# An attention and feed-forward kernel: an earlier load of x, and ScalarE's high halves behind the exponents

## The reference

```python
x = x + xattn(layernorm(x), ctx, ctx, Wq, Wk, Wv, Wo)     # 16 heads of 32, rotary q and k, softmax over 120 keys
x = x + ffn(layernorm(x), w_gate, w_up, w_down)           # 512 -> 1536 -> 512

def ffn(x, w_gate, w_up, w_down):
    x = act_qdq(x)                                        # 16-bit quantize and back, one scale for the tensor
    up = act_qdq(x @ lpbq_dequant(w_up).T)                # 4-bit weights in blocks of 32
    gate = act_qdq(x @ lpbq_dequant(w_gate).T)
    gate = act_qdq(gate * fixed_qdq_u16(sigmoid(gate)))
    return act_qdq(gate * up) @ lpbq_dequant(w_down).T
```

## Time and profile before

| | us |
|---|---|
| median of three runs | 2319.28 |
| the profiled execution | 2318.47 |
| its span, first to last instruction | 2316.7 |
| TensorE busy | 2199.2 |
| VectorE busy | 1686.2 |
| ScalarE busy | 1330.6 |
| GpSimd busy | 704.9 |

### The profile page before, as it was taken

The page is one execution under the profiler, slowest core; times in us unless marked ns, Lnnn a source line. Parts: engine busy times, 40 slices in busy tenths (PEclk is TensorE's granted clock), DMA queues, the critical chain, the costliest instruction groups (busy, mean ns, idle before and its releaser), DMA issues. The chain is left out here.

```text
span 2316.7 us, 31161 instructions
## 1 busy us (share of the span) xinstructions
PE 2199.2 (95%) x12037; PEld 970.5 (42%) x12037; DVE 1686.2 (73%) x1690; ACT 1330.6 (57%) x1299; POOL 704.9 (30%) x655
## 2 busy tenths in 40 slices
PE   5898999999988899999999999999998799999999
PEld 3443333333332444444444444444443344444444
DVE  7656899898975766445543598888888887778773
ACT  3345666666644232222322787877877777777772
POOL 3444675766663311000100364444444000000000
PEclk9899999999999999999999999999999899999999
DMA  6334686877777568888875898877876565655552
GB/s 193 95 103 116 179 194 173 193 173 192 170 159 178 164 215 256 272 246 253 250 227 180 292 329 311 299 286 286 293 284 259 189 234 211 236 226 205 205 217 91
DMA packets 287190, 500.14 MB, mean 216 GB/s; under 512 B 187980, under 2 KB 190284, under 8 KB 250172
## 3 DMA queue, kind: packets, MB, share of 16 engines
q1 hardware_dynamic: 287036, 498.10, 68.1%
HBM read 247.75 MB, written 186.58 MB: 187 GB/s over the span
## 5 line engine op out<-in xcount | busy, mean ns | idle before, releaser
L1698 PE MATMUL banks<-XB,W 128*128 128x512 f16 x2304 | 500.1, 380 | 2.3 <-ACT XB L1724 2.3
L1698 PE MATMUL banks<-XB,WT 128*128 128x512 f16 x2304 | 497.4, 379 | 0.0
L2164 PE MATMUL banks<-W,OH 128*128 128x512 f16 x2256 | 487.1, 379 | 3.6 <-DVE OH L2266 3.6
L1718 ACT ACTIVATE OB<-banks,uns 128x512 f32<-128x512 f32 x384 | 255.7, 684 | 393.2 <-PE banks L1698 390.4
L1698 PEld LDWEIGHTS banks<-XB,W 128*128 128x128 f16 x2304 | 225.9, 98 | 276.1 <-issue 5.1
L1698 PEld LDWEIGHTS banks<-XB,WT 128*128 128x128 f16 x2304 | 225.4, 98 | 271.8
L2164 PEld LDWEIGHTS banks<-W,OH 128*128 128x128 f16 x2256 | 220.7, 98 | 270.0 <-DVE OH L2266 4.0
L1985 POOL TENSOR_TENSOR PR<-GS,OB 128x2048 f32<-128x2048 f32 x46 | 220.5, 4794 | 257.6 <-ACT OB L1718 247.6
L1807 DVE TENSOR_REDUCE amx<-OB 128x1 f32<-128x2048 f32 x48 | 109.7, 2285 | 239.8 <-ACT OB L1718 239.8
L752 PE MATMUL banks<-XC,AH 128*128 128x512 f16 x768 | 179.2, 385 | 5.4 <-POOL AH L1510 3.7
L693 PE MATMUL banks<-XD,WQ 128*128 128x512 f16 x768 | 177.0, 380 | 2.2 <-ACT WQ L878 0.8
(11 more groups left out here) (272 smaller groups left out, 2866.2 us busy)
## 6 DMA issues: line engine op xcount, KB each, us to landing
g_s<-OB SPq DMA_DIRECT2D x48, 1024.0 KB, 6.0
GL<-g_s SPq DMA_DIRECT2D x48, 1024.0 KB, 7.3
up_s<-OB SPq DMA_DIRECT2D x48, 1024.0 KB, 4.9
XA<-up_s SPq DMA_DIRECT2D x32, 1024.0 KB, 9.3
gq_s<-GQ SPq DMA_DIRECT2D x48, 512.0 KB, 4.7
XD<-gq_s SPq DMA_DIRECT2D x48, 512.0 KB, 6.7
XA<-in_x SPq DMA_DIRECT2D x16, 1024.0 KB, 6.3
QW<-QE SPq DMA_DIRECT2D x128, 128.0 KB, 3.0
```

What stands on the lines that cost most here:

```text
L1698: t = e.matmul(pk[:].rearrange("p (j t) -> p j t", j=4), WT[w][:, ot, wa, kk, :], XB[i % 2][:, xa, :, kk, :], start=(kk == 0 and wa == 0 a ...
L1718: e.activation(OB[n % 3][:, r, :], bank[(k + 4) % 8][:], ACT.Copy, scale=uns[:, 12 * w + ot:12 * w + ot + 1]).then_inc(s_ev, 1)
L2164: t = e.matmul(pk[:].rearrange("p (r n) -> p r n", r=4), OH[i % 2][:, a, ot, j * 128:(j + 1) * 128], WD[:, :, c, wa, o4, :], start=(ot == ...
```

## The change

For steps s >= 16, five things move:

- SyncE issues the load of x in c = 1, ahead of the first DMA transpose, and no longer in c = 2 behind the second one.
- VectorE takes two of the four statistics of x early in c = 3, ahead of the rotary sum, and the other two where all four stood.
- ScalarE writes the second of a step's two high halves of AH right behind the next step's exponents.
- The gate tile's high half is written one step later, in c = 2 ahead of the copy of the turned maxima (MT).
- Its low half on GpSimd moves one step later too, behind that step's low halves of AH, and its store one step later. For the last tile the store stays in the last step.

```diff
+                if s >= 16 and c == 1 and b + 2 < B:
+                    sp_x_load(e, b + 2)
                 for nb in [1] if s == 2 else x_at(s, 2):
                     sp_x_turn(e, nb, 0)
...
                 for nb in x_at(s - 1, 2) if s > 16 else []:
                     sp_x_turn(e, nb, 1)
-                if c == 2 and 2 <= b + 2 < B:
+                if s < 16 and c == 2:
                     sp_x_load(e, b + 2)
...
-                    if w_step(k) + 6 == s:
+                    if min(w_step(k) + 7, NSTEP - 1) == s:
                         e.wait_ge(s_wl, k + 1)
                         e.dma_start(w_home(k), w_hl).then_inc(s_ws, 16)
...
+        def act_a_high(e, u):
...
+            e.activation(AH[nb % 2][:, 0, nc_, :], A[:, u % 6, :], ACT.Copy).then_inc(s_ah, 1)
...
                     e.activation(P[0:SK], PB[0:SK, 0:4, :], ACT.Exp, scale=SM_SCALE).then_inc(s_p, 1)
+                for u in normal_at(s - 1)[1:] if s > 16 else []:
+                    act_a_high(e, u)
...
+                for k in range(12):
+                    if w_step(k) + 6 == s:
...
+                        e.activation(w_hl[:, 0, :], w_ld[k % 2], ACT.Copy).then_inc(s_wh, 1)
...
+                for u in normal_at(s)[:1] if 16 <= s < NSTEP - 1 else normal_at(s):
+                    act_a_high(e, u)
...
+        def dve_x_sums(e, b, part):
...
+            for j in range(2 * part, 2 * part + 2):
                 e.bn_stats(st1[b % 2][:, j, :], X[:, j, :]).then_inc(s_lst, 1)
...
+                for nb in x_at(s, 0) if s >= 16 else []:
+                    dve_x_sums(e, nb, 0)
                 if 1 <= s <= NU:
                     dve_rope_add(e, ROT["q", s - 1])
...
-                    if w_step(k) + 5 == s:
+                    if w_step(k) + 6 == s:
                         e.wait_ge(s_wh, k + 1)
                         e.tensor_tensor(w_hl[:, 1, :], w_ld[k % 2], w_hl[:, 0, :], ALU.subtract).then_inc(s_wl, 1)
```

More of the change, by code:

```diff
@@ L953, in act_largest @@
             e.activation(MT[:], BQ_, ACT.Copy, scale=(QS * QS if 4 * b >= HALF else 1.0) / MS).then_inc(s_mte, 1)
+        def act_a_high(e, u):
+            nb, nc_ = divmod(u, 4)
+            e.wait_ge(s_an, u + 1)
+            if nb >= 2:
+                e.wait_ge(s_o, 4 * (nb - 2) + 4)
+            elif u == 0:
+                e.wait_ge(s_v, 16)
+                e.wait_ge(s_ct, 32)
+            e.activation(AH[nb % 2][:, 0, nc_, :], A[:, u % 6, :], ACT.Copy).then_inc(s_ah, 1)
         def act_attention(e):
@@ L1002, in act_attention @@
                     act_x_high(e, nb)
+                for k in range(12):
+                    if w_step(k) + 6 == s:
+                        e.wait_ge(s_wx, 2 * k + 2)
+                        if k >= 1:
+                            e.wait_ge(s_ws, 16 * k)
+                        e.activation(w_hl[:, 0, :], w_ld[k % 2], ACT.Copy).then_inc(s_wh, 1)
                 if s == 1:
@@ L1031, in act_attention @@
                     act_x_high(e, nb)
-                for k in range(12):
-                    if w_step(k) + 5 == s:
[L1035 to L1038, removed]
             u = NU - 5
@@ L1142, in dve_rope_add @@
                 e.tensor_tensor(KR[g][:, r, :], KR[g][:, r, :], QW[n % 2][:, 0:4 * SK], ALU.add).then_inc(s_radd, 1)
-        def dve_x_stats(e, b):
+        def dve_x_sums(e, b, part):
             e.wait_ge(s_x, 16 * (b + 1))
@@ L1147, in dve_x_stats @@
                 e.wait_ge(s_lmv, b - 1)
-            for j in range(4):
+            for j in range(2 * part, 2 * part + 2):
                 e.bn_stats(st1[b % 2][:, j, :], X[:, j, :]).then_inc(s_lst, 1)
+        def dve_x_stats(e, b):
+            if b < 6:
+                dve_x_sums(e, b, 0)
+            dve_x_sums(e, b, 1)
             e.wait_ge(s_lst, 4 * b + 4)
```

## The result

The kernel after took 2335.19 us, the median of nine runs (2324.24 to 2348.65), against 2319.28 before: ratio 1.0069, 95% interval 1.0047 to 1.0091. It is slower by 16 us where 5.6 us faster were forecast, and lies outside the range. One of these nine took 5925 us and one of the kernel before beside them 6128; the ratios leave these two out.

A forecast was written before the change was run, and what follows sets the result against it. It took a loop through VectorE, SyncE and GpSimd, not TensorE, to pace attention's rounds. Ten rounds win 6.8 us, the tail loses 1.2: 5.6 us off, so 2313.7 us against 2319.28, range 2301 to 2326.

The forecast's parts named there:

- the new loop: Attention's rounds of four steps: 34.5 + 2.6 = 37.1 us against 37.78, so 0.68 us won per round, 6.8 in ten.
- d: SyncE, first transpose and the swap behind it: wait 2.6 us more for the load's bytes; bounds 0 and 6.3.
- the tail's 1.2 us: Attention's end: the last gate tile's store up to 6.7 us late, 5.5 covered, so 1.2 us lost; bounds 0 and 6.7.
- The loop: Attention's rounds: reciprocals, RB fetch, transpose, swap, GpSimd's product, MX and statistics set the pace, 37.5 us against 37.78 measured.
- The hold: SyncE's queue in c = 1: the first transpose's hold of 5.2 us should be near 8 after the change.
- VectorE's gain: VectorE in c = 3: half the statistics, 1.24 us, and the wait for the load, 1.72, go: 2.96 us per round.
- The sign: Attention's rounds: VectorE's gain of 2.96 us exceeds the added wait of 2.6, so each round gets shorter.
- Break-even: Whole kernel: the gain, rounds less the tail's loss, is zero at an added wait d of 3.16 us.
- The rest of the loop: Attention's rounds: the 37.5 us loop changes only by 2.96 us taken off and 2.6 added.
- The second rival: First transpose in c = 1: the load starts after RB drains, d 4.5 us, loop 39.0, total 2333 us; chance 0.17.

The follow-up runs named there:

- after_again: The changed kernel, unaltered, timed again in a later set of nine executions against the kernel before: median 2335.93 us, ratio 1.0060.
- load: Kernel before with only the load of x moved ahead of the first transpose and the statistics split: 2325.98 us, ratio 1.0033.
- low_wait: Kernel before with no load moved; SyncE's first transpose in c = 1 also waits for VectorE's two low halves: 2318.9 us, ratio 0.9993.
- half_load: Kernel before with split statistics and 0.5 MB of the load ahead of the first transpose, 0.5 MB where the load was: 2314.01 us, 0.9986.
- after_turn: Changed kernel with the load of x directly behind the first transpose instead of ahead of it: 2326.29 us, ratio 1.0025 to the kernel before.
- load_ah: Changed kernel without the gate tile's move: 2333.01 us, ratio 1.0076 to the kernel before.
- after_tail: Changed kernel with the last gate tile's three pieces back where they stood before: 2327.35 us, ratio 1.0039 to the kernel before.
- load_gate: Changed kernel without the move of AH's second half: 2338.45 us, ratio 1.0098 to the kernel before.
- load_turn: Kernel before with split statistics and the load of x directly behind the first transpose of c = 1: 2314.53 us, ratio 0.9985.

## Why the prediction was wrong, step by step

The step that failed first is the subtraction in "the new loop", 34.5 + 2.6 against 37.78. Its gain, 2.96 us, measured 2.4, its cost d, 2.6 us, measured 3.0 with the load alone, and the difference changed its sign. Two more terms were missing or too small: TensorE's clock was not in the sum, and the tail's 1.2 us were 5.7. In after_again's profile the ten rounds took 12.7 us more than before, 8.2 of them in slow steps, and the tail 5.8.

- **The loop: right in what it is made of.** In the kernel after no wait for the exponents and none of the statistics for the load was left in the rounds, and the waits for MX stood at the start of c = 0, as forecast. The hold, 7.5 us in the mean, is near the 8 forecast. But only five of ten c = 0 steps took 8.85 us, and the rounds 40.35 (39.05 in after_again) instead of 37.1.
- **VectorE's gain, 2.96 us: too large.** Measured, by the rest in before and load, is 12.3 - 9.9 = 2.4. I took 1.72 us of waiting for the load from one round, which was about the longest there is. VectorE's waits for it, 247 to 625 us, were

```profile
DVE st L1149 <- DMA XA<-in_x: 11.0, 8, 1.7
```

  which is 1.1 a round; with 1.24 for the two statistics that makes 2.34.
- **The added wait d, 2.6 us by bytes: the mechanism right, the size too small.** With the load alone d was 3.0; without the round behind its one slow step the way is 28.3 instead of 28.5 us, and d 2.8. I said that the load's own issue falls inside the wait; but the load itself first waits for VectorE's low halves (their buffer is the one it overwrites), a wait that cost nothing behind the second transpose. low_wait shows that this holds up nothing as long as only the transpose is late; with the load it is the bytes that start late. It is a candidate for the 0.5 us above the bytes; half_load, which waits for less, stayed at 1.4 against 1.3.
- **The sign.** 2.96 - 2.6 = +0.36 had been added to a loop of 37.5 us that already stood 0.28 below the measured one (the way of the two rounds used was 24.8, over all rounds it is 25.5), so 0.28 of the 0.68 won per round (with rounding) came from comparing a modelled loop with a measured one; with the measured 2.4 - 3.0 = -0.6 the round grows. Break-even was put at d = 3.16; with the measured gain it is 2.4, below the 2.6 that I took myself.
- **The rest of the loop taken as rigid: wrong in the kernel after.** There the way grew by 3.6 (after_again) to 4.5 us. By the table, of the 1.5 beyond the load alone 0.7 lie in a later RB fetch, 0.4 in the hold and 0.5 in the swap; after_again's 0.6 are spread. In the rows above the swap of c = 0 stands in front of the RB fetch and waits for query rows that the slow step delays. Over after_again's ten rounds the way behind its five slow steps is 30.6 us in the mean, behind the other five 28.0, about the 28.3 of the load alone; in after_turn it is 30.1 and 28.0, in load_ah 30.2 and 28.1. In the first profile of the kernel after there is no such difference (30.3 and 30.4), though its RB fetches come 4.5 and 3.1 us behind the reciprocals. So a slow step goes with a longer next round in most of these kernels; no run lowered the clock alone to show that it is the cause.
- **The clock: not in the prediction at all.** Five steps in the profiled execution lost 1.6 to 3.0 us each, 13.2 of the 25.7 us that its ten rounds lost; in after_again five times 1.6, 8.2 of 12.7.
- **The tail, 1.2 us: too small by 4.5.** I set the store's delay against the 5.5 us between the sums' fetch and the reciprocals as if they were free. They are the time of the fetch itself and what follows it, and cover nothing that stands ahead of the fetch. The sums were sent right behind the late store and transpose, at 759.27. A wait of 4.67 us and a slow set of products followed, 5.7 us in all; after_tail takes it away.
- **The second rival** named about this time, 2333 us, and its 12.2 us for ten rounds are near after_again's 12.7. That is luck in the number: its reason was another, a hold of 4.5 us more; the measured one is 1.5 to 2 more, with a later issue, a smaller gain, and the clock.
- What stays open: why AH's half costs 0.4% without the gate tile's move, alone (1.0037) and with the load (load_ah 1.0076, load 1.0033), and why load_gate has the highest median of all; its profiled execution was the shortest of its six and doesn't tell. With them, how the 16 us of the median divide among loop, clock and tail is open; the profiles divide only their own executions.

## What to carry to other kernels

Take the size of a wait that a change removes from the sum over its rounds, not from the round that shows it best; where two nearly equal terms are subtracted, this decides the sign. A transfer that is issued sooner takes its own waits and its bytes along to everything queued behind it: read an issue and a hold behind it as one sum. Here half of the transfer, or all of it one place further back in the queue, won 3.8 and 3.3 us where the whole load in front of the transpose lost 9.7. And where waits are gathered into one, ask what TensorE's clock does behind it: here waits near 1 us left it alone, and those of 2.9 to 3.3 us each cost 1.6 us or more on top.

## What the runs showed of the hardware

- Behind each of TensorE's waits of 3.49 us and more in the steady rounds of all kernels its granted clock was below 1.00 in the products that followed, and the step 1.6 to 3.0 us longer on top of the wait. Between 1.97 and 3.35 us it went both ways: slow behind 1.99, 2.20 and 3.10 us in after_again, at full clock behind 2.60 and 2.67 there and behind 3.35 in after_tail. Behind shorter ones the clock stayed up. Waits of one length cost differently, and the kernel with the longest of them also scatters more (2324 to 2349 us in nine executions) than the kernel before (2316 to 2327).
- A DMA transpose on SyncE's queue, behind the fetches of RB at a DMA share of 0.26, let go at a time that did not depend on its own issue: issued 2.7 us later, at 487.41 instead of 487.68. With a load of 0.5 or 1 MB directly in front, it let go 0.2 to 0.6 us ahead of that load's landing in all 80 cases.
- The sixteen loads of 1 MB took 8.0 us from issue to landing in the median instead of 6.3, and those of the ten rounds, which stand behind such fetches, 8.6. Issued behind the transpose (load_turn), they took 6.2.
